# Graph network kernel: the last half's residual is summed in PSUM, and ScalarE and VectorE normalize one set of four graphs each

## What is computed

```
h = L0(x)                    # two graph convolutions, then LSTMs over windows of 1 to 4 nodes
x = layernorm(x + h)         # the residual and the row normalization that are changed
A_hat = normalized adjacency
z = (A_hat x) W1^T + b1      # in the same stage: "mix", then "z"
z = relu(batchnorm(z))       # batch statistics over ALL graphs
y = batchnorm(z W2^T + b2)   # again over all graphs
out = layernorm(x + y)
```

## Time and profile before

| | |
|---|---|
| median of three runs | 805.26 us (805.22 to 805.91) |
| the profiled execution | 805.59 us, of it 803.8 us between the first and last instruction (the span) |
| TensorE busy | 774.3 us, 96% |
| VectorE busy | 716.6 us, 89% |
| ScalarE busy | 597.0 us, 74% |
| GpSimd busy | 114.3 us, 14% |
| TensorE's granted clock | 0.996 of full speed over the span |

### The profile page before, as it was taken

The page is one execution under the profiler, slowest core; times in us unless marked ns, Lnnn a source line. Parts: engine busy times, 40 slices in busy tenths (PEclk is TensorE's granted clock), DMA queues, the critical chain, the costliest instruction groups (busy, mean ns, idle before and its releaser), DMA issues.

```text
span 803.8 us, 15599 instructions
## 1 busy us (share of the span) xinstructions
PE 774.3 (96%) x4968; PEld 530.8 (66%) x4968; DVE 716.6 (89%) x1826; ACT 597.0 (74%) x1186; POOL 114.3 (14%) x125
## 2 busy tenths in 40 slices
PE   8999999999999999999999999999999988899995
PEld 5666777777767776777777777767766655344542
DVE  4787989999999999999999999999999989688996
ACT  4876777777777777777777778777868754796598
POOL 0000000000000000000000000000000001487695
PEclk9999999999999999999999999999999999999998
DMA  5010001010101010101010101010000000154245
GB/s 201 28 52 1 1 28 53 28 52 28 53 29 53 26 52 26 52 26 52 26 52 26 52 26 52 27 53 28 27 27 28 27 27 27 52 170 171 81 181 209
DMA packets 17693, 44.44 MB, mean 55 GB/s; under 512 B 2032, under 2 KB 3184, under 8 KB 17520
## 3 DMA queue, kind: packets, MB, share of 16 engines
q1 hardware_dynamic: 17504, 43.81, 15.3%
q10 hardware_dynamic: 144, 0.07, 0.0%
HBM read 27.09 MB, written 16.78 MB: 55 GB/s over the span
## 4 chain that ended last, share of the span: by engine, by line
PE 78%; DVE 10%; ACT 5%; issue 3%; DMA 1%; SPq 1%; POOL 1%; ACTq 0%; DVEq 0%; POOLq 0%
PE gate_bank L952 14%; PE gate_bank L953 14%; PE gate_bank L967 6%; PE gate_bank L977 6%; PE gate_bank L1024 4%; PE back_bank L906 3%; PE front_bank L862 3%; ACT z L1165 3%; PE front_bank L879 3%; PE front_bank L867 3%; PE front_bank L873 3%; PE gate_bank L936 3%; PE gate_bank L937 3%; PE gate_bank L938 3%; PE gate_bank L960 3%
## 5 line engine op out<-in xcount | busy, mean ns | idle before, releaser
L952 PE MATMUL gate_bank<-h_hi,w_hi 128*128 128x256 f16 (+2 forms) x528 | 161.9, 307 | 4.4 <-DVE h_lo L1382 2.9
L953 PE MATMUL gate_bank<-h_hi,w_lo 128*128 128x256 f16 (+2 forms) x528 | 161.7, 306 | 0.0
L1108 ACT ACTIVATE gate_i<-gate_bank,lstm_bias 128x512 f32<-128x512 f32 (+2 forms) x176 | 99.7, 567 | 61.5 <-PE gate_bank L977 32.1
L1108 ACT ACTIVATE gate_o<-gate_bank,lstm_bias 128x512 f32<-128x512 f32 (+2 forms) x176 | 100.2, 569 | 30.9 <-PE gate_bank L977 20.8
L967 PE MATMUL gate_bank<-h_lo,w_hi 128*128 128x256 f16 (+2 forms) x384 | 115.8, 301 | 0.0
L755 POOL TENSOR_TENSOR rstd<-veps,neg_half 128x8 f32<-128x8 f32 x15 | 26.3, 1752 | 628.3 <-DVE veps L1304 628.3
L952 PE MATMUL gate_bank<-s_hi,w_hi 128*128 128x256 f16 (+2 forms) x384 | 112.7, 302 | 1.4 <-DVE s_hi L1379 1.3
L1365 DVE SCALAR_TENSOR_TENSOR gate_f<-gate_o,gate_f 128x512 f32<-128x512 f32 (+2 forms) x176 | 94.8, 539 | 20.6 <-ACT gate_f L1114 19.6
L953 PE MATMUL gate_bank<-s_hi,w_lo 128*128 128x256 f16 (+2 forms) x384 | 112.6, 301 | 0.0
L1114 ACT ACTIVATE gate_f<-cell 128x512 f32<-128x512 f32 (+2 forms) x176 | 89.7, 510 | 28.1 <-DVE cell L1362 14.3
L1108 ACT ACTIVATE gate_g<-gate_bank,lstm_bias 128x512 f32<-128x512 f32 (+2 forms) x176 | 99.6, 566 | 0.5
(11 more groups left out here) (261 smaller groups left out, 1730.1 us busy)
## 6 DMA issues: line engine op xcount, KB each, us to landing
x_kept<-normed_sb SPq DMA_DIRECT2D x16, 512.0 KB, 2.6
z<-x_kept SPq DMA_DIRECT2D x16, 512.0 KB, 3.8
rows_sb<-in_x SPq DMA_DIRECT2D x15, 512.0 KB, 3.3
x_front<-in_x SPq DMA_DIRECT2D x15, 512.0 KB, 4.1
out<-z SPq DMA_DIRECT2D x15, 512.0 KB, 3.1
z<-in_wr SPq DMA_DIRECT2D x1, 1536.0 KB, 7.4
x_front<-in_x SPq DMA_DIRECT2D x2, 256.0 KB, 3.4
out<-z SPq DMA_DIRECT2D x2, 256.0 KB, 2.5
```

Source lines behind the costliest of these rows:

```text
L952: mm(dst, w[0], v[0], start=start, stop=False)
L953: mm(dst, w[1], v[0], start=False, stop=False)
L1108: ins = activation(acts[gate][h][:, 0:n], gate_bank[h][bank_of(job, gate)][:, 0:n], ACT.Tanh if gate == "g" else ACT.Sigmoid, bias=lstm_bi ...
```

## The change

Only the last half's back part is changed, and one detail of all the others.

- TensorE first puts `x_front` into the bank by a product with the f32 identity (two products of 512 columns, f32) and then adds the tokens onto it. For that the tokens must arrive unscaled: `ident16` now holds 2^-14 instead of 1. The sum of input and tokens so stands in PSUM, and VectorE has no residual step in the last half.
- In the other 15 halves `ident16` is the same tile, so their residual step becomes a plain addition (`tensor_tensor`) in place of a scaled one (`scalar_tensor_tensor`).
- The rows of the last half now stand in `front_bank` (set 0) and `gate_bank11` (set 1); the mixes go to `gate_bank10` and `gate_bank12`.
- The moments are those that the final stage uses (`row_steps`, five small instructions, mean with its sign turned).
- ScalarE normalizes set 0, from PSUM, as x * rstd + (-mean * rstd), for which GpSimd makes the product -mean * rstd; VectorE normalizes set 1, from PSUM. Each has a semaphore of its own.
- Both sets' statistics and moments come first on VectorE, then one early aggregate, then set 1's normalization, then the other aggregate.
- `STAY_WARM`, the number of unread products in each of two places, is 18, not 20.

```diff
-        last_bank = [front_bank, *gate_bank[1]]
-        last_mix_bank = last_bank[0:2]
+        last_row_bank = [front_bank, gate_bank[1][1]]
+        last_mix_bank = [gate_bank[1][0], gate_bank[1][2]]
...
-        STAY_WARM = 20
+        STAY_WARM = 18
...
@@ block.gpsimd
                 nc.gpsimd.tensor_tensor(rstd[0][:, at], veps[0][:, at], neg_half[:, at], ALU.pow).then_inc(last_rstd, 1)
+                if n == 0:
+                    pool.wait_ge(last_rstd, 1)
+                    nc.gpsimd.tensor_tensor(mean_rstd[0][:, at], comb[0][:, 2, at], rstd[0][:, at], ALU.mult
+                                            ).then_inc(last_shift, 1)
...
@@ block.tensor
-            wait(pe, (LSTM_JOBS[-1], "low"), GROUPS - 1, 1)
             wait(pe, ("mix1", "low", 1), GROUPS - 1, 1)
             for n in range(2):
+                if n:
+                    wait(pe, (LSTM_JOBS[-1], "act", "g"), GROUPS - 1, 1)
+                mm(last_row_bank[n][:], ident[:], x_front[:, n, :], start=True, stop=False, skip_group_check=True)
+            wait(pe, (LSTM_JOBS[-1], "low"), GROUPS - 1, 1)
+            for n in range(2):
                 for b in range(4):
-                    to = last_mix_bank[n][:, b * P:(b + 1) * P]
-                    mm(to, h_hi[1][:, :, 4 * n + b], ident16[:], start=True, stop=False)
-                    ins = mm(to, h_lo[1][:, :, 4 * n + b], ident16[:], start=False, stop=True)
+                    to = last_row_bank[n][:, b * P:(b + 1) * P]
+                    mm(to, h_hi[1][:, :, 4 * n + b], ident16[:], start=False, stop=False, skip_group_check=True)
+                    ins = mm(to, h_lo[1][:, :, 4 * n + b], ident16[:], start=False, stop=(b == 3), skip_group_check=True)
                 ins.then_inc(last_tokens, 1)
...
@@ block.scalar
+            act.wait_ge(last_shift, 1)
+            act.wait_ge(sem_kept, 16 * (HALVES - 1))
+            for b in range(4):
+                ins = activation(normed[:, 0, b * P:(b + 1) * P], last_row_bank[0][:, b * P:(b + 1) * P], ACT.Identity,
+                                 bias=mean_rstd[0][:, b:b + 1], scale=rstd[0][:, b:b + 1])
+            ins.then_inc(last_normed[0], 1)
...
@@ block.vector
-            ve.tensor_copy(ident16[:], ident[:])
+            ve.tensor_scalar(ident16[:], ident[:], 1.0 / H_SCALE, None, ALU.mult)
...
-                    ins = ve.scalar_tensor_tensor(out=rows[:, n, :], in0=back_to(g, h, n)[:], scalar=1.0 / H_SCALE,
-                                                  in1=rows[:, n, :], op0=ALU.mult, op1=ALU.add)
+                    ins = ve.tensor_tensor(rows[:, n, :], back_to(g, h, n)[:], rows[:, n, :], ALU.add)
...
+            dve.wait_ge(last_tokens, 1)
+            row_stats(last_row_bank[0], bn[0], 0).then_inc(last_moments, 1)
+            last_steps(0)
+            dve.wait_ge(last_tokens, 2)
+            row_stats(last_row_bank[1], bn[0], 1).then_inc(last_moments, 1)
+            last_steps(1)
+            early_aggregate(0)
             dve.wait_ge(sem_kept, 16 * (HALVES - 1))
+            dve.wait_ge(last_rstd, 2)
+            for b in range(4):
+                last = ve.tensor_scalar(normed[:, 1, b * P:(b + 1) * P], last_row_bank[1][:, b * P:(b + 1) * P],
+                                        comb[0][:, 2, 4 + b:5 + b], rstd[0][:, 4 + b:5 + b], ALU.add, ALU.mult)
+            last.then_inc(last_normed[1], 1)
+            early_aggregate(1)
             for n in range(2):
-                dve.wait_ge(last_rstd, n + 1)
-                normalize(rows, normed, comb[0], rstd[0], n).then_inc(last_normed, 1)
-            for n in range(2):
-                early_aggregate(n)
                 dve.wait_ge(last_mixed, n + 1)
                 high, low = agg(n)
                 ve.tensor_tensor(low, last_mix_bank[n][:], high, ALU.subtract).then_inc(last_low, 1)
```

More of the change, by code:

```diff
@@ L526, in gnn_lstm_kernel @@
         last_tokens = sem("last_tokens")
-        last_residual = sem("last_residual")
         last_moments = sem("last_moments")
         last_rstd = sem("last_rstd")
-        last_normed = sem("last_normed")
+        last_shift = sem("last_shift")
+        last_normed = [sem(f"last_normed{n}") for n in range(2)]
         last_mix = sem("last_mix")
@@ L648, in last_z_bank @@
         def last_z_bank(n):
-            return last_bank[(0, 2, 1, 3)[n]]
+            return (last_row_bank + last_mix_bank)[n]
         def half_of(dram, g, h):
@@ L992, in _ @@
             for n in range(2):
-                pe.wait_ge(last_normed, n + 1)
+                pe.wait_ge(last_normed[n], 1)
                 for i in range(4):
@@ L1394, in _, with row_steps @@
             dve.wait_ge(sem_x, 16 * HALVES)
-            for n in range(2):
-                at = slice(4 * n, 4 * n + 4)
[L1397 to L1401, removed]
+            def row_steps(bn_t, comb_t, veps_t, step):
+                mean_e, m2_e, mean_o, m2_o = (bn_t[:, :, n] for n in (1, 2, 4, 5))
+                apart, m2, minus_mean = (comb_t[:, n, :] for n in range(3))
+                if step == 0:
+                    ve.scalar_tensor_tensor(out=m2, in0=m2_e, scalar=P * EPS, in1=m2_o, op0=ALU.add, op1=ALU.add)
+                    return ve.tensor_tensor(apart, mean_e, mean_o, ALU.subtract)
+                if step == 1:
+                    ve.scalar_tensor_tensor(out=minus_mean, in0=apart, scalar=-0.5, in1=mean_o, op0=ALU.mult,
+                                            op1=ALU.subtract)
+                    return ve.scalar_tensor_tensor(out=veps_t, in0=apart, scalar=0.25, in1=apart, op0=ALU.mult,
+                                                   op1=ALU.mult)
+                return ve.scalar_tensor_tensor(out=veps_t, in0=m2, scalar=1.0 / P, in1=veps_t, op0=ALU.mult,
+                                               op1=ALU.add)
@@ L1508, in _ @@
                                     op0=ALU.mult, op1=ALU.add).then_inc(sem_bn2, 1)
-            def row_steps(bn_t, comb_t, veps_t, step):
-                mean_e, m2_e, mean_o, m2_o = (bn_t[:, :, n] for n in (1, 2, 4, 5))
-                apart, m2, minus_mean = (comb_t[:, n, :] for n in range(3))
-                if step == 0:
-                    ve.scalar_tensor_tensor(out=m2, in0=m2_e, scalar=P * EPS, in1=m2_o, op0=ALU.add, op1=ALU.add)
-                    return ve.tensor_tensor(apart, mean_e, mean_o, ALU.subtract)
-                if step == 1:
-                    ve.scalar_tensor_tensor(out=minus_mean, in0=apart, scalar=-0.5, in1=mean_o, op0=ALU.mult,
-                                            op1=ALU.subtract)
-                    return ve.scalar_tensor_tensor(out=veps_t, in0=apart, scalar=0.25, in1=apart, op0=ALU.mult,
-                                                   op1=ALU.mult)
-                return ve.scalar_tensor_tensor(out=veps_t, in0=m2, scalar=1.0 / P, in1=veps_t, op0=ALU.mult,
-                                               op1=ALU.add)
             def row_terms(t, u, scaled_next, sets=range(2), seen=0):
```

6 lines of the change are left out of this document (4 added, 2 removed).

## The result

The changed kernel takes 804.25 us (median of 12 runs, 803.47 to 805.65) against 805.55 us for the kernel before (12 runs, 805.13 to 807.2). The ratio is 0.9982 with a 95% interval of 0.9974 to 0.9990: it is 1.3 us faster by the medians and 1.45 us by the ratio (0.8 to 2.1 by its interval). The gain is real, but under the 0.2% from which the prediction calls a change faster. The prediction was 803.9 us, or 1.4 us less than before.

The account below looks back on a forecast made before the run. The prediction took the last half's latency chain before the `Relu` pass as the bound. Terms +0.22 - 0.73 - 0.77 - 0.06 + 0.25 - 0.33 = -1.4 us gave 803.9 us against 805.26, range 803.2 to 804.9.

Parts of the forecast that it names:

- tokens late by the identity products: Last half's back part: two f32 products on TensorE delay VectorE's start on set 0's tokens from 676.54 to 676.76, +0.22 us.
- set 0's statistics to set 1's, 2.32 to 1.55: VectorE, last half: set 1's residual and one small instruction leave the chain, -0.77 us.
- copy to low part: Last half: second aggregate no longer precedes set 1's low part, which follows ScalarE's copy after 0.63 instead of 0.96, -0.33 us.
- low part to the end of the statistics, 3.18: Last half: VectorE's final stretch from set 1's low part runs without a gap and stays 3.18 us.
- What bounds the kernel: Between 676.5 and 691 us the stage is pure latency; each us off its chain is a us off the kernel.
- GpSimd's extra product hidden: Last half: set 1's power is due at S + 3.26, exactly when GpSimd is free; nothing to spare, cost 0.
- ScalarE's four at 1.50: ScalarE's four normalizing instructions for set 0 take 1.50 us, as in the final stage's rows.
- Both ways end within 0.05 us of each other: End of last half's statistics: last bank readable at S + 10.08, VectorE there about S + 10.12; any delay on either shows.
- Rival 1: Last half: ScalarE's four, unhidden weight loads or GpSimd's second power run late; gain only 0.7, 804.6 us; chance 0.20.
- rival 2: Identity products cost nothing, hidden in TensorE's 1.34 us of idleness; gain 1.6 and 0.1 elsewhere, 803.6 us; chance 0.12.
- Rival 3: Idle TensorE drops to 1.2 GHz, so mixes and `z` products take twice as long; +3.2 us, 808.5 us; chance 0.02.
- Rival 4: Nothing gained: the stage isn't the bound, the `Relu` pass or a transfer waits for something else; 805.3 us; chance 0.04.

Follow-up runs that it names:

- moved product: The changed kernel with set 1's identity product issued behind set 0's tokens: 804.14 us, ratio to before 0.9984, last stage 14.06 us.

## Why the prediction was right

The mechanism and the size held, term by term. The terms as predicted, and as the rows of after give them against those of before:

| step | predicted | measured |
|---|---|---|
| tokens late by the identity products | +0.22 | +0.17 (VectorE starts 1.07 after `h_lo`, 0.90 before) |
| set 0's residual | -0.73 | -0.73 |
| set 0's statistics to set 1's, 2.32 to 1.55 | -0.77 | -0.77 (676.62 to 678.17) |
| set 1's statistics to its power | -0.06 | -0.04 (678.17 to 679.90) |
| power to normalization, 1.09 | 0 | +0.03 (679.90 to 681.02) |
| set 1's normalization from PSUM | +0.25 | +0.26 (681.02 to the mix at 682.44) |
| copy to low part | -0.33 | -0.33 (683.64 to 684.27) |
| low part to the end of the statistics, 3.18 | 0 | +0.05 (684.27 to 687.50) |
| sum | -1.4 | -1.36 |

The 0.05 in the last row is VectorE's subtraction at 0.69 instead of 0.63 us. From the end of the statistics to the `Relu` pass it is 2.21 us instead of 2.20, which makes the 1.35.

- *What bounds the kernel.* Shown: the terms taken off VectorE's chain add up to what the stage lost, and what follows the `Relu` pass kept its length (112.65 us before, 112.79 after; 112.59 to 112.79 over all twelve profiles). TensorE's work is in that chain only with set 1's mix (1.20 us until ScalarE's copy). The wait before the `Relu` pass is 1.48 us as before (1.49).
- *GpSimd's extra product hidden.* Shown by the 0.28 us that the second power waits for VectorE.
- *ScalarE's four at 1.50.* Measured 1.51. The estimate from the Trainium skill (ScalarE: Activation LUTs, What ACT_TABLE_LOAD costs) was 1.64. The trace's figure was the right one for PSUM; from SBUF, with the residual on VectorE, the four took 1.65. The 0.1 us that the prediction adds to the whole for it is too much: an extra 0.14 us on set 0 lies within the 0.2 us of slack measured with ScalarE's work doubled.
- *Both ways end within 0.05 us of each other.* Half right. They are near each other, but doubling set 0's step showed 0.2 us of slack; "any delay on either shows" was wrong for set 0. With that step doubled, the last `z` product starts 12.00 us into the stage instead of 10.70, so 0.07 of the 1.37 us is already gone: VectorE's second aggregate holds set 0's low part anyway. From that product to the end of the statistics it is then 1.11 us instead of 1.25, another 0.14: VectorE gets to the last bank later than TensorE is ready with it, not just 0.04 later as I had reckoned (S + 10.12 against S + 10.08).
- *Rival 1 (one way late)* did not occur; *rival 2 (identity products free)* did not either, 0.17 of 0.22 us was paid, and a version in which it is not paid exists. *Rival 3 (clock)* is a real mechanism with 3 to 4 times less of a price than I gave it (1.26 against 4.6 us): I let the half clock last through all mixes and `z` products, while it was back within 4 us. My condition for it was wrong too: "idleness of some 2.3 us is safe" came from one row, and near 656 us the clock fell 1.9 us after the last product in one profile (last section). *Rival 4* is excluded, since the `Relu` pass came 1.35 us earlier after `h_lo` and all behind it with it.
- *Where the forecast and the medians differ.* 803.9 against 804.25 is 0.35 us, of which 0.3 lies in the kernel before: its median is 805.26 over three runs, 805.55 over twelve. Against that the gain is 1.3, forecast 1.4.

How the gain splits, each part taken off the changed kernel: 1.03 us is the residual summed in PSUM; 0.24 is ScalarE's normalization together with the moved aggregates (14.40 without both, 14.41 without the aggregates alone). The plain additions and the two fewer unread products bring nothing. The remaining 0.08 of the 1.35 fits the one small instruction less: with the residual on VectorE in both, from set 0's statistics to set 1's it is 2.25 us (677.11 to 679.36) in the kernel with the five instructions and 2.32 in the kernel before. I didn't try it apart.

## What to carry to other kernels

At a point where all engines wait for a global statistic, count the chain and not the busy shares: an idle TensorE can do an addition that sits on VectorE's chain, even as an f32 product that takes longer than the addition it replaces. Handing a step to a slower, idle engine paid here only because something that was in the way moved into the hole. Unread products that keep the clock up stand themselves in TensorE's queue: when work ahead of them grows, check that they don't hold up the next real product.

## What the runs showed of the hardware that I had not expected

The same 2.89 us of idleness near 656 us was followed by a fall of TensorE's granted clock in some executions and not in others, with the same instructions before it. Windows of the changed kernel (columns as above):

```profile
656.00:658.00 2.00, 0.00 (x0) 0.00 (x0) 1.38 (x4) 0.48 (x1) 0.00 (x0) 1.00 0.00 0
658.00:659.00 1.00, 0.81 (x7) 0.73 (x8) 0.96 (x6) 0.27 (x1) 0.00 (x0) 0.91 0.00 0
659.00:662.00 3.00, 3.00 (x16) 2.05 (x15) 2.29 (x11) 1.37 (x4) 1.64 (x1) 0.50 0.00 0
662.00:663.00 1.00, 0.97 (x8) 0.55 (x6) 0.99 (x4) 0.42 (x2) 0.00 (x0) 0.88 0.00 0
```

And of the kernel with ScalarE's work doubled, which is the same program up to there:

```profile
657.00:658.00 1.00, 0.00 (x0) 0.00 (x0) 0.93 (x4) 0.00 (x0) 0.00 (x0) 0.53 0.00 0
658.00:663.00 5.00, 4.98 (x24) 3.46 (x25) 3.69 (x17) 1.72 (x4) 1.64 (x1) 0.50 0.00 0
```

By these windows the clock fell 1.9 us after the last product in this profile, within the idle stretch, and in the changed kernel's 0.6 us after TensorE had started again. So no length of idleness parts the executions with a fall from those without. From the end of the idle stretch to the end of `h_lo` it took 16.88 to 16.89 us where the clock stayed full (before, plain additions, moved product, both sets on VectorE), 17.36 in the changed kernel's profile, 17.51 or 17.52 in four others and 18.22 in the one with the longest fall. The profile of before happened to have no fall and that of after had one, 0.47 us; the last stage alone is free of it.

A second source of scatter is at the start: TensorE waits there for the second half's `x_front`, and its first product with it starts between 16.51 and 17.24 us. All that follows shifts with it: from that product to GpSimd's first power it is 78.9 to 79.0 us in eleven of the twelve profiles. Before it is 17.24, after 16.68, which is 0.56 us in favour of the profile of after and about makes up for its 0.47.

The twelfth is the one with the aggregates put back. There TensorE waited longest, 1.78 us, and its clock then fell to half from about 17.6 to 21 us (the mean of 12 to 30 us is 0.91, where it is 1.00 in the others):

```profile
16.92 1.29 PE L867 MATMUL front_bank<-adjT_sb,x_front 128*128 128x128 f32 x7 [1.78 <-DMA x_front<-in_x]
...
19.51 0.63 PE L941 MATMUL gate_bank<-h_hi,wih_hi 128*128 128x512 f32 x1
```

```profile
12.00:30.00 18.00, 14.83 (x77) 11.06 (x75) 11.42 (x20) 13.01 (x20) 0.00 (x0) 0.91 0.27 107
```

Products of 512 columns follow each other every 0.42 us there and every 0.23 us from 21 us on. It is this fall and not the wait itself that made the execution slow: with plain additions TensorE started at 16.93, and the first power came at 95.87; here it started at 16.92, and the power came at 97.41. The fifteenth power came there at 662.48 instead of 660.0 to 660.9. Between the first power and the last of the planned part it is 564.5 to 564.6 us in seven profiles and 565.0 to 565.2 in the five in which the clock had fallen well ahead of the last. So in these twelve profiles nearly all scatter comes from the start and from the stretch near 656 us; I did not try to mend the start.
